# GpSimd's two waits for VectorE, before the factors and before the decay product, taken out of a 64-sequence decoder layer

## The chip, the cores and the metric

The kernel runs on one core of a Trainium2 chip. The metric is the device time of one launch in microseconds (us); lower is better. One launch computes the layer for all 64 sequences.

## The reference

Each of 64 sequences has x of 256 tokens x 256 features and a context of 120 tokens. The layer is three blocks, each with a residual and a layer norm after it:

```python
x = _layernorm(x + mamba2(x))                 # in-projection, conv, SSD scan with decay matrix, gate, out-projection
x = _layernorm(x + cross_attention(ctx, x))   # 8 heads of 64; keys and values from [context; x]
x = _layernorm(x + ffn(x))
...
# ffn
gf = _global_net(x.mean(axis=1))
out = x
for _ in range(3):
    tf = _coupling_net(out)                   # one number per token
    coupling = BASE_COUPLING + adaptive_range * (0.7 * gf + 0.3 * tf - 0.5) * 2.0
    out = out + coupling * _twist(out)        # _twist: a signed permutation of the four feature quarters
```

All data is float32. What matters here: attention ends in a division by the softmax sums (`oT * invT`), then the product with `wo`; the three cycles of the ffn are linear in x, so the kernel folds them, once the three couplings are known, into two factors per token, `out = of_x * x + of_tw * twist(x)`.

## The kernel before, in words

The four compute engines and the DMA queue each have a hand-written list of steps, and semaphores tie them together. The lists are software-pipelined over the sequences: in one turn of the main loop (61 turns, p = 2 to 62) sequence m = p is projected and scanned, a = p - 1 finishes its scan block and begins attention, f = p - 2 is in the middle of attention, f - 1 finishes attention and does its ffn, f - 2 gets its output. A turn takes some 56 us. Before and after the loop the same steps stand in lists of their own.

Names used below, by engine:

- TensorE: `turn(s, n)` (L455) transposes the probabilities of one head and token tile into a PSUM bank; `w_o(s, i)` (L482) is the output product of attention, 8 matmuls per token tile. Both take their banks from `ring_b`, which has only two, 4 and 5, in turn. In the loop the order is `turn(f, 0)`, `w_o(f - 1, 0)`, `w_o(f - 1, 1)`, `turn(f, 1)`. So `w_o(f - 1, 1)` needs the bank of `turn(f, 0)` back, and that is freed by VectorE's `turn_out(f, 0)`.
- VectorE: `divide(s, d)` (L1773) multiplies `oT` by the inverse sums, both from SBUF, in two halves; `out_x(s, i)` (L1860) and twice `out_tw(s, i, k)` (L1869) form the layer's output in `out_sb` from x2 and the factors; `turn_out` (L1764) copies a transposed tile out of PSUM. The order at the place of the change is `divide(f - 1, 0)`, `top(f, 1)` (the row maxima, L1741), `divide(f - 1, 1)`, `out_x(f - 2, 1)`, `out_tw(f - 2, 1, 0)`, `out_tw(f - 2, 1, 1)`, `turn_out(f, 0)`, `x2_raw(f - 1, 0)` (L1783).
- ScalarE: `t_col` (L1066) is the last output of the coupling net, `G` (L941) the product C B^T of the scan, and L948 and L949 make the decay matrices `Lm`, one head at a time.
- GpSimd: `masked` (L2458) masks `Lm`; `factors(s)` (L2541 to L2558) is ten tiny operations of 128x2 that make `of_x`, `of_tw`, `of_minus`; `times_g(s, q)` (L2471) multiplies two heads of `Lm` by `G`, both from SBUF, 128x384 each. The order is `masked(m, 0)` to `masked(m, 3)`, `factors(f - 1)`, `times_g(m, 0)`, `times_g(m, 1)`, and, at the head of the next turn, `times_g(a, 2)`, `times_g(a, 3)`.

One thing to watch: the turns of the engines' loops are not cut at the same moment. GpSimd's `factors(f - 1)` at the end of its turn is what VectorE's `out_x(f - 2, 1)` reads near the start of its next turn, and the second half of `divide(f)` that GpSimd's wait names is VectorE's `divide(f - 1, 1)` of its next turn. So the place of the change is one stretch of time, in which VectorE divides, waits for the factors, and forms the output.

The two waits are optional arguments: `factors(s, divided=...)` waits for `d_o`, which VectorE's two divisions raise, ahead of L2547; `times_g(s, q, summed=...)` waits for `d_out[1]`, which `out_x` and the two `out_tw` of token tile 1 raise. Neither protects data: what GpSimd touches after them is not what VectorE reads or writes before them.

Of the kernel before, what the change touches and what calls it, by code (L numbers as in the profile page):

```python
# [34 lines left out]
def decoder_layer(nc, x, xT, ctx_in, par_in, w_in, w_out, wq, wkv, wo, cw1, cw2, cw3, cw4, gw1, gw2, gw3, out):  # L35
# [25 lines left out]
    with es:  # L61
# [171 lines left out]
        def live(s):  # L233
            return 0 <= s < NSEQ
# [3 lines left out]
        def _(e):  # L238
# [220 lines left out]
            def values(s, d):  # L459
                if not live(s):  # L460
                    return
                b = bank_of["val", s, d] = take(ring_b)
                pe.wait_ge(a_v, 3 * s + 3)
                pe.wait_ge(a_tn, 8 * s + 4 * d + 4)
                pe.wait_ge(d_tn, 8 * s + 4 * d + 4)
                for c in (2 * d, 2 * d + 1):
                    at = c % 2 * L
                    for j, (_, m) in enumerate(JT):
                        for k in range(2):
                            h = 2 * c + k  # L470
                            t = mm(banks[b][k * HD:(k + 1) * HD, at:at + L], V[0:m, j, h * HD:(h + 1) * HD],  # L471
                                   probT[0:m, (8 * s + h) % HP, j, :], start=j == 0, stop=j == len(JT) - 1)
                    t.then_inc(p_val, 1)
                freed[b] = [(a_o, 2 * s + d + 1)]
# [987 lines left out]
        def _(e):  # L1462
# [3 lines left out]
            def row_stats(s, name, src, rows, done, first=0):  # L1466
                stats, _, _, _ = stat[name]
                e.bn_stats(stats[0:rows, first, :], src).then_inc(done, 1)
# [969 lines left out]
        def _(e):  # L2438
# [12 lines left out]
            def masked(s, q):  # L2451

                if not live(s):
                    return
                po.wait_ge(cum_in, 32 * s + 32)
                for c0 in (0, L):
                    pair = Lm[:, 2 * q:2 * q + 2, c0:c0 + P]
                    t = e.affine_select(out=pair, in_=pair, compare_op=ALU.is_ge, fill=MINUS, base=0, pattern=[[0, 2], [1, P]],  # L2458
                                        channel_multiplier=-1)
                t.then_inc(l_mask, 1)  # L2460

            def times_g(s, q, summed=None):

                if not live(s):
                    return
                if summed is not None:
                    po.wait_ge(d_out[1], 3 * summed + 3)
                po.wait_ge(a_G, s + 1)
                for h in (2 * q, 2 * q + 1):
                    po.wait_ge(a_dec, 8 * s + h + 1)  # L2470
                    t = tt(Lm[:, h, :], Lm[:, h, :], G[:, :], ALU.mult)  # L2471
                t.then_inc(l_Lm, 1)

            def gated(s, q):
                if not live(s):
                    return
                po.wait_ge(d_yD, 4 * s + q + 1)
                po.wait_ge(d_gate, 2 * s + 2)
                po.wait_ge(p_out, s)
                po.wait_ge(a_sq, 4 * s)  # L2480
                tt(g[:, q, :], yD[:, q, :], gate[:, q, :], ALU.mult).then_inc(l_g, 1)  # L2481

            def squares(s):
                if not live(s):
                    return
                po.wait_ge(a_sq, 4 * s + 4)
                tt(sq[:, 0:2, :], sq[:, 0:2, :], sq[:, 2:4, :], ALU.add).then_inc(l_sum, 1)
                po.wait_ge(l_sum, 2 * s + 1)
                tt(sq[:, 0, :], sq[:, 0, :], sq[:, 1, :], ALU.add).then_inc(l_sum, 1)

            def inv_rms(s):
                if not live(s):
                    return
                po.wait_ge(d_msv, s + 1)
                po.wait_ge(d_x1p, 2 * s)
                tt(rms[:, :], ms[:, :], minus_half[:, 0:TT], ALU.pow).then_inc(l_rms, 1)

            def mix(s):

                if not live(s):  # L2500
                    return
                _, mv, ve_, rs = stat["mix"]
                po.wait_ge(d_mix, 8 * s + 4)
                ts(ve_[:, 0:TT], mv[:, :, 1], EPS, None, ALU.add).then_inc(l_mix, 1)
                ts(ve_[:, TT:2 * TT], mv[:, :, 1], 1.0 + EPS, EPS * EPS, ALU.mult, ALU.add).then_inc(l_mix, 1)
                po.wait_ge(l_mix, 3 * s + 2)
                tt(rs[:, :], ve_[:, :], minus_half[:, :], ALU.pow).then_inc(l_mix, 1)

            def context(s):
                if live(s):  # L2510
                    rstd(s, "ctx", 1, J, d_ctx, l_ctx)

            def att(s, i):
                if live(s):
                    rstd(s, "att", 1, P, d_att[i], l_att[i], first=i)

            def ffn(s, i):
                if live(s):
                    rstd(s, "ffn", 1, P, d_ffn[i], l_ffn[i], first=i)

            def twist(s):

                if not live(s):
                    return
                po.wait_ge(d_f, FD * s + 3)
                tt(h_a[:, :, :], h_a[:, :, :], cpl[:, 0, :].unsqueeze(1).broadcast_to([P, KT, L]), ALU.mult).then_inc(l_tw, 1)  # L2526
                po.wait_ge(l_tw, 2 * s + 1)
                tt(h_b[:, :, :], h_b[:, :, :], h_a[:, :, :], ALU.subtract).then_inc(l_tw, 1)

            def factors(s, divided=None):  # L2530


                if not live(s):
                    return
                n = 8 * s
                po.wait_ge(d_out[0], 3 * s)
                po.wait_ge(d_out[1], 3 * s)
                for k in range(2):
                    po.wait_ge(c_in[k], 16 * (s + 1))
                c, d, e_ = (c_col[:, k, :] for k in range(3))  # L2540
                tt(cd[:, :], c, d, ALU.mult).then_inc(l_fac, 1)  # L2541
                tt(c_d[:, :], c, d, ALU.add).then_inc(l_fac, 1)
                po.wait_ge(d_base, s + 1)
                po.wait_ge(a_f, FA * s + 16)
                if divided is not None:
                    po.wait_ge(d_o, 2 * divided + 2)
                ts(e_, t_col[:, :], tf_gain[:, :], c_cyc[:, :], ALU.mult, ALU.add).then_inc(l_fac, 1)  # L2547
                po.wait_ge(l_fac, n + 3)
                ts(one_cd[:, :], cd[:, :], -1.0, 1.0, ALU.mult, ALU.add).then_inc(l_fac, 1)
                tt(e_sum[:, :], e_, c_d[:, :], ALU.mult).then_inc(l_fac, 1)  # L2550
                po.wait_ge(l_fac, n + 5)
                tt(e_one[:, :], e_, one_cd[:, :], ALU.mult).then_inc(l_fac, 1)
                po.wait_ge(l_fac, n + 6)
                tt(of_x[:, :], one_cd[:, :], e_sum[:, :], ALU.subtract)
                tt(of_tw[:, :], c_d[:, :], e_one[:, :], ALU.add).then_inc(l_fac, 1)
                po.wait_ge(l_fac, n + 7)
                ts(of_x[:, :], of_x[:, :], 1.0, None, ALU.add)
                ts(of_minus[:, :], of_tw[:, :], -1.0, None, ALU.mult).then_inc(l_fac, 1)  # L2558
# [44 lines left out]
            for p in range(2, NSEQ - 1):  # L2603
                f, a, m = p - 2, p - 1, p
                times_g(a, 2)
                times_g(a, 3)
                gated(a, 0)
                gated(a, 1)
                gated(a, 2)
                att(f - 1, 1)  # L2610
                gated(a, 3)
                att(f - 1, 0)
                squares(a)
                context(a)
                ffn(f - 2, 1)
                inv_rms(a)
                mix(a)
                twist(f - 1)
                ffn(f - 2, 0)
                masked(m, 0)  # L2620
                masked(m, 1)
                masked(m, 2)
                masked(m, 3)
                factors(f - 1, divided=f)
                times_g(m, 0, summed=f - 1)
                times_g(m, 1)
            last = NSEQ - 1
            times_g(last - 1, 2)
# [15 lines left out]
            masked(last, 1)  # L2644
            masked(last, 2)
            masked(last, 3)
            factors(last - 3, divided=last - 2)
            times_g(last, 0, summed=last - 3)
            times_g(last, 1)
            times_g(last, 2)  # L2650
            att(last - 2, 1)
# [12 lines left out]
            ffn(last - 3, 0)  # L2664
            att(last - 1, 1)
            ffn(last - 3, 1)
            factors(last - 2, divided=last - 1)
            twist(last - 1)
            ffn(last - 2, 0)
            att(last, 0)  # L2670
            att(last, 1)
            ffn(last - 2, 1)
            factors(last - 1, divided=last)
            ffn(last - 1, 1)
            twist(last)
            ffn(last - 1, 0)
# [235 lines left out]
```

## Time and profile before

| | |
|---|---|
| median of 3 runs | 3686.03 us (3682.52 to 3687.17) |
| the profiled execution | 3687.81 us, span 3685.6 us |
| TensorE clock granted, mean | 0.991 |
| TensorE matmul busy | 3613.6 us, 98% of the span |
| VectorE busy | 3246.4 us, 88% |
| ScalarE busy | 3072.9 us, 83% |
| GpSimd busy | 1788.0 us, 49% |
| chain of work that ended last | 93% TensorE, 3% VectorE, 1% each ScalarE, issue, SyncE's queue, DMA, GpSimd |

A row of a timeline tells when an instruction started, how long it took, and, in brackets, how long its engine sat idle before it and who ended that. A row of the waits tells who waited for whom, the sum over the span, how many times, and the longest.

### The profile page before, as it was taken

To read this page: it belongs to the slowest core of one execution; us is meant where nothing else is said; L and a number is where in the kernel's file an instruction comes from. 1 tells how busy PE (TensorE), PEld (TensorE's weight loads), DVE (VectorE), ACT (ScalarE), POOL (GpSimd) and SP (SyncE) were. 2 spreads that over 40 slices of the span, in tenths; PEclk is the share of its full clock that TensorE was granted. 3 is DMA by queue.
4 is the path that set the end of the run, shared out by engine and by line. 5 is a ranking of instruction groups with operands and counts; after the bars stand their busy time and mean duration, and the time that the engine had idled before them with its cause. 6 is when DMAs were issued, how large, how long until landed. Compare 5 with 4: busy or idle time off the path is not lost.

```text
span 3685.6 us, 79670 instructions
## 1 busy us (share of the span) xinstructions
PE 3613.6 (98%) x26752; PEld 3085.0 (84%) x26752; DVE 3246.4 (88%) x7970; ACT 3072.9 (83%) x7559; POOL 1788.0 (49%) x3084
## 2 busy tenths in 40 slices
PE   5999999999999999999999999999999999999997
PEld 4888888888888888888888888888888888888885
DVE  7888988988988989889889889889898898898884
ACT  5788888888888888888888888888888888888884
POOL 4355454454554554554544545545545545445442
PEclk8999999999999999999999999999999999999998
DMA  3212212112122122122121121221221221211210
GB/s 100 59 37 67 59 42 67 52 49 67 39 63 64 37 67 64 37 67 58 43 67 53 48 67 39 63 65 37 67 64 37 67 60 42 67 55 46 67 34 21
DMA packets 312358, 203.28 MB, mean 55 GB/s; under 512 B 55056, under 2 KB 310928, under 8 KB 311952
## 3 DMA queue, kind: packets, MB, share of 16 engines
q1 hardware_dynamic: 311952, 198.20, 18.7%
q8 instruction: 215, 3.52, 0.4%
q14 instruction: 191, 1.56, 0.1%
HBM read 180.17 MB, written 17.96 MB: 54 GB/s over the span
## 4 chain that ended last, share of the span: by engine, by line
PE 93%; DVE 3%; ACT 1%; issue 1%; SPq 1%; DMA 1%; POOL 1%; POOLq 0%; DVEq 0%; ACTq 0%
PE psum L263 35%; PE psum L455 10%; PE psum L471 9%; PE psum L443 8%; PE psum L350 6%; PE psum L482 6%; PE psum L518 5%; PE psum L338 5%; PE psum L524 2%; PE psum L533 2%; PE psum L322 1%; PE psum L495 1%; PE psum L383 1%; PE psum L361 1%; PE psum L545 1%
## 5 line engine op out<-in xcount | busy, mean ns | idle before, releaser
L1015 ACT ACTIVATE prob<-psum,nmax 128x376 f32<-128x376 f32 x1024 | 588.7, 582 | 36.0 <-DVE nmax L1741 35.0
L2471 POOL TENSOR_TENSOR Lm<-Lm,G 128x384 f32<-128x384 f32 x512 | 497.3, 1011 | 81.8 <-DVE out_sb L1869 68.8
L1741 DVE TENSOR_REDUCE nmax<-psum 128x2 f32<-128x752 f32 x512 | 472.8, 934 | 44.2 <-PE psum L443 39.4
L455 PE MATMUL psum<-ident,prob 128*128 128x128 f32 (+1 forms) x3072 | 486.4, 278 | 3.1 <-DVE probT L1764 1.7
L455 PEld LDWEIGHTS psum<-ident,prob 128*128 128x128 f32 (+1 forms) x3072 | 354.8, 141 | 87.0 <-issue 46.5
L1493 DVE SCALAR_TENSOR_TENSOR u<-psum,par,u 128x255 f32<-128x255 f32 (+5 forms) x960 | 408.2, 467 | 12.0 <-ACT u L914 1.5
L2458 POOL TENSOR_SCALAR_AFFINE_SELECT Lm<-Lm 128x256 f32<-128x256 f32 x512 | 193.0, 416 | 375.7 <-DMA Lm<-cum_row 375.5
L2526 POOL TENSOR_TENSOR h_a<-h_a,cpl 128x512 f32<-128x512 f32 x64 | 83.0, 1297 | 594.0 <-DVE h_pre L1852 594.0
L471 PE MATMUL psum<-probT,V 128*64 128x256 f32 (+1 forms) x3072 | 360.5, 383 | 0.4 <-ACT probT L1025 0.4
L263 PE MATMUL psum<-x_hi,w_in_hi 128*128 128x256 f32 (+1 forms) x1152 | 344.8, 299 | 13.0 <-DVE w_in_lo L1897 7.6
L263 PE MATMUL psum<-x_hi,w_in_lo 128*128 128x256 f32 (+1 forms) x1152 | 325.4, 282 | 0.0
L263 PE MATMUL psum<-x_lo,w_in_hi 128*128 128x256 f32 (+1 forms) x1152 | 324.7, 282 | 0.0
L1025 ACT ACTIVATE probT<-psum 128x384 f32<-128x384 f32 x512 | 254.7, 498 | 79.6 <-PE psum L455 72.2
L1764 DVE COPY probT<-psum 128x384 f32<-128x384 f32 x512 | 281.4, 550 | 30.4 <-PE psum L455 30.2
L471 PEld LDWEIGHTS psum<-probT,V 128*64 128x64 f32 (+1 forms) x3072 | 208.6, 136 | 110.9 <-ACT probT L1025 0.4
L948 ACT ACTIVATE Lm<-Lm,ncum 128x256 f32<-128x256 f32 x512 | 264.8, 517 | 2.6 <-DVE ncum L1605 1.9
L263 PEld LDWEIGHTS psum<-x_hi,w_in_hi 128*128 128x128 f32 (+1 forms) x1152 | 214.0, 186 | 29.6 <-issue 21.2
L350 PE MATMUL psum<-w_out_sb,g 128*128 128x256 f32 x1024 | 236.8, 384 | 1.3 <-DVE dt_a L1507 1.3
L482 PE MATMUL psum<-wo_sb,oT 128*128 128x256 f32 x1024 | 235.5, 381 | 1.7 <-DVE probT L1764 1.4
L518 PE MATMUL psum<-h,cw_sb 128*128 128x256 f32 x768 | 209.3, 395 | 10.2 <-ACT h L1058 8.4
L1015 ACT ACTIVATION_READ_ACCUMULATOR prob<-psum,nmax 128x1 f32 x1024 | 218.7, 214 | 0.0
L2481 POOL TENSOR_TENSOR g<-xc,gate 128x256 f32<-128x256 f32 x256 | 206.5, 826 | 19.5 <-DVE xc L1628 19.4
(227 smaller groups left out, 11668.6 us busy)
## 6 DMA issues: line engine op xcount, KB each, us to landing
Lm<-cum_row SPq DMA_DIRECT2D x64, 1024.0 KB, 5.2
Lm<-cum_row SPq DMA_DIRECT2D x64, 512.0 KB, 6.6
invT<-inv_row SPq DMA_DIRECT2D x256, 128.0 KB, 3.0
xT_sb<-in_xT SPq DMA_DIRECT2D x64, 256.0 KB, 2.7
x_sb<-in_x SPq DMA_DIRECT2D x64, 256.0 KB, 5.8
result<-out_sb SPq DMA_DIRECT2D x64, 256.0 KB, 2.4
inv_row<-inv_t SPq DMA_DIRECT2D x512, 1.0 KB
ctx_sb<-in_ctx SPq DMA_DIRECT2D x64, 120.0 KB, 6.4
```

Source lines behind the costliest of these rows:

```text
L263: t = mm(dst, a, b, start=n == 1, stop=n == 3 * KT)
L350: t = mm(banks[b][:, i * D:(i + 1) * D], g[:, c, i * P:(i + 1) * P], w_out_sb[:, c, :], start=c == 0, stop=c == CT - 1)
L443: t = mm(banks[at[k]][:, 0:NK], q_[r, c, i * P:(i + 1) * P], k_[r, c, :], start=m == 0, stop=m == 2)
L455: t = tr(banks[b][0:m, j * P:(j + 1) * P], prob[:, r, j0:j0 + m], ident[:, :])
L471: t = mm(banks[b][k * HD:(k + 1) * HD, at:at + L], V[0:m, j, h * HD:(h + 1) * HD], probT[0:m, (8 * s + h) % HP, j, :], start=j == 0, stop= ...
L482: t = mm(banks[b][:, 0:D], oT[:, c, i * P:(i + 1) * P], wo_sb[:, c, :], start=c == 0, stop=c == CT - 1)
L518: t = mm(b[:, 0:L], cw2_sb[:, k, :], h1[:, k, :], start=k == 0, stop=k == KT - 1)
L1015: act(prob[:, r, :], b[:, 0:NK], ACT.Exp, bias=nmax[:, n:n + 1], accum_out=psum_row[:, n:n + 1]).then_inc(a_exp, 1)
L1493: stt(u[0:rows, c, d:L], src[:, 0:L - d], prm("conv_w", 4 * c + 3 - d, slice(0, rows)), u[0:rows, c, d:L], ALU.mult, ALU.add).then_inc(don ...
L1741: e.tensor_reduce(nmax[:, 2 * n:2 * n + 2], psum[:, b:b + 2, 0:NK], AX.X, ALU.max, negate=True).then_inc(d_max, 1)
L1764: cp(probT[:, (8 * s + 2 * c + k) % HP, :, i * P:(i + 1) * P], b[:, 0:len(JT) * P].rearrange("p (j t) -> p j t", j=len(JT))).then_inc(d_tn, 1)
L2471: t = tt(Lm[:, h, :], Lm[:, h, :], G[:, :], ALU.mult)
```

## The change

GpSimd no longer waits for VectorE's two divisions inside `factors`, nor for VectorE's output sum before the first `times_g`. This is done at all five calls of `factors` that had the wait (one of them in the loop) and at both calls of `times_g` (one in the loop). No instruction is added, removed or moved on any engine; the definitions keep their optional arguments, unused.

```diff
@@ gpsimd, main loop
                 masked(m, 3)
-                factors(f - 1, divided=f)
-                times_g(m, 0, summed=f - 1)
+                factors(f - 1)
+                times_g(m, 0)
                 times_g(m, 1)
@@ gpsimd, after the loop
-            factors(last - 3, divided=last - 2)
-            times_g(last, 0, summed=last - 3)
+            factors(last - 3)
+            times_g(last, 0)
             times_g(last, 1)
@@
-            factors(last - 2, divided=last - 1)
+            factors(last - 2)
             twist(last - 1)
@@
-            factors(last - 1, divided=last)
+            factors(last - 1)
             ffn(last - 1, 1)
```

## Rows read from the trace of the kernel before

**Rows 1.** Busy time by engine, from 200 to 3400 us: us, busy us (instructions) of each.

```profile
200.00:3400.00 3200.00, 3196.59 (x23846) 2735.05 (x23844) 2875.25 (x7077) 2731.86 (x6734) 1591.94 (x2740) 1.00 0.19 55
```

**Rows 2.** Waits over the span: who <- whom, us in total, times, longest us.

```profile
DVE out_sb L1860 <- POOL of_minus L2558: 139.4, 61, 6.4
PEld psum L482 <- DVE probT L1764: 8.3, 23, 1.0
```

**Rows 3.** Timeline of VectorE in an ordinary turn: start us, us.

```profile
2147.27 0.69 DVE L1773 TENSOR_TENSOR oT<-oT,invT 128x512 f32<-128x512 f32 x1
...
2150.58 0.35 DVE L1869 SCALAR_TENSOR_TENSOR out_sb<-x,of_tw,out_sb 128x128 f32<-128x128 f32 x1
2150.85 0.34 DVE L1869 SCALAR_TENSOR_TENSOR out_sb<-x,of_minus,out_sb 128x128 f32<-128x128 f32 x1
2151.11 0.55 DVE L1764 COPY probT<-psum 128x384 f32<-128x384 f32 x1
```

**Rows 4.** Timeline of GpSimd in the same turn.

```profile
2148.18 0.34 POOL L2547 TENSOR_SCALAR c_col<-t_col,tf_gain,c_cyc 128x2 f32<-128x2 f32 x1 [3.06 <-DVE oT L1773]
...
2149.93 0.23 POOL L2558 TENSOR_SCALAR of_minus<-of_tw 128x2 f32<-128x2 f32 x1
2151.28 5.83 POOL L2471 TENSOR_TENSOR Lm<-Lm,G 128x384 f32<-128x384 f32 x6 [1.12 <-DVE out_sb L1869]
```

**Rows 5.** Timeline of ScalarE in the same turn.

```profile
2147.14 0.26 ACT L1066 ACTIVATE t_col<-psum,half_b 128x2 f32<-128x2 f32 x1
...
2149.55 0.51 ACT L941 ACTIVATE G<-psum 128x384 f32<-128x384 f32 x1
```

**Rows 6.** Timeline of TensorE: the output product in this turn and the next.

```profile
2150.20 3.62 PE L482 MATMUL psum<-wo_sb,oT 128*128 128x256 f32 x16
...
2206.17 3.62 PE L482 MATMUL psum<-wo_sb,oT 128*128 128x256 f32 x16
```

**Rows 7.** Timeline of a turn in which VectorE is late, and the next output product.

```profile
2936.14 0.55 DVE L1764 COPY probT<-psum 128x384 f32<-128x384 f32 x1
...
2934.41 1.89 PE L482 MATMUL psum<-wo_sb,oT 128*128 128x256 f32 x8
2936.74 1.99 PE L482 MATMUL psum<-wo_sb,oT 128*128 128x256 f32 x8 [0.44 <-DVE probT L1764]
...
2991.12 3.62 PE L482 MATMUL psum<-wo_sb,oT 128*128 128x256 f32 x16
```

**Rows 8.** Timeline of a turn in which TensorE and ScalarE are ahead of VectorE.

```profile
1814.33 0.35 DVE L1869 SCALAR_TENSOR_TENSOR out_sb<-x,of_tw,out_sb 128x128 f32<-128x128 f32 x1
...
1814.86 0.55 DVE L1764 COPY probT<-psum 128x384 f32<-128x384 f32 x1
...
1813.08 0.51 ACT L941 ACTIVATE G<-psum 128x384 f32<-128x384 f32 x1
...
1813.72 3.73 PE L482 MATMUL psum<-wo_sb,oT 128*128 128x256 f32 x16
```

**Rows 9.** Timeline near the end: an out_tw beside GpSimd's gated products.

```profile
3564.55 2.18 POOL L2481 TENSOR_TENSOR g<-xc,gate 128x256 f32<-128x256 f32 x3
...
3565.35 0.78 DVE L1869 SCALAR_TENSOR_TENSOR out_sb<-x,of_tw,out_sb 128x128 f32<-128x128 f32 x1
```

**Rows 10.** Timeline near the end: a times_g operation beside VectorE's x_lo.

```profile
3500.86 1.50 POOL L2471 TENSOR_TENSOR Lm<-Lm,G 128x384 f32<-128x384 f32 x1
...
3500.80 0.69 DVE L1487 TENSOR_TENSOR x_lo<-xT_sb,x_hi 128x512 fp32r<-128x512 f32 x1 [0.41 <-ACT x_hi L881]
```

**Rows 11.** Timeline: a tiny operation of factors beside one of VectorE.

```profile
461.85 0.47 POOL L2542 TENSOR_TENSOR c_d<-c_col 128x2 f32<-128x2 f32 x1
...
461.85 0.41 DVE L1541 TENSOR_TENSOR C_st<-th,C_st 16x256 fp32r<-16x256 f32 x1
```

**Rows 12.** Timeline: GpSimd's sum of squares, released by ScalarE's last square.

```profile
1828.68 0.41 ACT L955 ACTIVATE gate<-g 128x256 f32<-128x256 f32 x1
...
1829.17 1.28 POOL L2487 TENSOR_TENSOR gate<-gate 128x512 f32<-128x512 f32 x1 [0.74 <-ACT gate L955]
```

## The prediction

> **What bounds the kernel now.** First the busy times of the long middle of the run: TensorE is busy for 3196.59 of 3200 us [rows 1]. It is the bound, and only what makes it wait costs or gains anything. Then the waits over the span [rows 2]: VectorE waits 139.4 us for the factors, in 61 places, and that looks like much. Little of it reaches TensorE: its weight loads wait 8.3 us in all for VectorE's `turn_out`, in 23 places. These 8.3 us are nearly all that a faster VectorE could give back here.
>
> Last the timelines of this one place. In an ordinary turn the output product starts at 2150.20 and takes 3.62 us for its 16 matmuls [rows 6]; `turn_out` ends at 2151.11 + 0.55 = 2151.66 [rows 3], 1.46 us after that start. The next output product starts at 2206.17 [rows 6], so this turn takes 55.97 us. In a late turn `turn_out` ends at 2936.69, 2.28 us after the product's start; the second eight matmuls wait for it and start 0.05 us later; the next product starts at 2991.12, a turn of 56.71 us [rows 7]: 0.74 us more. In a third turn `turn_out` ends 1814.86 + 0.55 - 1813.72 = 1.69 us after the start and the product takes 3.73 us, 0.11 more [rows 8]. So I read a **price list**: `turn_out` done 1.5 us after the product's start costs nothing, at 1.7 us it costs 0.11, and from there each us costs a us (2.28 gives about 0.7, and the turn shows 0.74). There is 0.2 us of slack at this spot, and the bound engine stands right behind it.
>
> **What the change does, step by step.** No instruction is added or moved, so there are only times of start to work out, on the ordinary turn.
>
> 1. *The factors start earlier.* Before, L2547 starts at 2148.18, after the division's end at 2147.27 + 0.69 = 2147.96 [rows 3, 4]. Its other inputs are ready with `t_col`, at 2147.14 + 0.26 = 2147.40 [rows 5]. It then starts soon after 2147.40, in the middle of the division, which began at 2147.27. A tiny operation of GpSimd that starts together with a VectorE operation on two SBUF inputs doesn't end until 0.06 us after it (0.47 against 0.41 us) [rows 11]. So L2547 ends at 2148.02 instead of 2148.52, 0.50 us earlier. Bounds: not held at all, it ends at 2147.40 + 0.34 = 2147.74 (0.78 earlier); held for its whole length of 0.34 after the division, it ends at 2148.30 (0.22 earlier). I take 0.50, the value of the nearest row. The division itself was started first, and I charge it nothing: no division beside it is seen, and its delay would be at most a tiny operation, 0.2 us, hidden in the factors' chain of 1.64 us that follows (2148.52 to 2150.16) [rows 4].
> 2. *VectorE's output sum follows.* The first `out_tw` starts 0.42 us after the factors' end (2150.58 against 2150.16) [rows 3, 4]. It would start at 2150.08, and with nothing in its way all behind it would be 0.50 us earlier.
> 3. *But `times_g` starts earlier too.* It needs `G`, ready at 2149.55 + 0.51 = 2150.06 [rows 5], and the end of the factors, now 2149.66. GpSimd's sum of squares starts 0.08 us after the ScalarE operation that releases it (1829.17 against 1829.09) [rows 12]; with that, `times_g` starts at 2150.14 instead of 2151.28 [rows 4]. Now it stands beside the two `out_tw`, which also read two SBUF inputs, and the trace shows what that does. An `out_tw` that started 0.11 us into a product of GpSimd, the second of three, which alone stands from 3565.24 to 3565.98, took 0.78 us instead of 0.35 and ended 0.15 us after that product [rows 9]. A `times_g` operation that started 0.06 us after VectorE's `x_lo` took 1.50 us instead of 5.83 / 6 = 0.97 [rows 4] and ended 0.87 us after it [rows 10]. So one holds the other, in both directions, and who starts first goes first.
> 4. *The ordinary turn.* The first `out_tw` (2150.08) is 0.06 us ahead of `times_g` (2150.14). It ends at 2150.43, `times_g` at +0.87 = 2151.30, the second `out_tw`, held meanwhile, at +0.15 = 2151.45. `turn_out` ends 0.47 us after that (2151.66 against 2151.19 before) [rows 3]: 2151.92, or 1.72 us after the product's start. By the price list, 0.11 us. The gain of 0.50 is used up by the hold.
> 5. *The turns where VectorE is behind.* In the third turn `G` is ready at 1813.59, so `times_g` could start at 1813.67, and the first `out_tw` only at 1814.33 - 0.50 = 1813.83 [rows 8]. GpSimd is first now, and both `out_tw` are held, each behind one operation: `times_g` ends at 1814.67, `out_tw` at 1814.82, the second `times_g` at 1815.69, the second `out_tw` at 1815.84, `turn_out` at 1816.31, which is 2.59 us after the product's start. That costs 0.11 + (2.59 - 1.72) = 1.0 us. With the times of each turn put in, 17 of the 61 are of this kind; one stands in the rows.
> 6. *The sum.* 44 x 0.11 + 17 x 1.0 = 21.8 us, in place of the 8.3 us that TensorE waits now: **+13.5 us**. Turns whose division is late today (rows 7) gain, and are in this difference. Against the profiled execution, 3687.8 + 13.5 = 3701.3; the median of the runs is 1.8 us below it, so **3699 us**.
>
> What else starts earlier: all eight `times_g` end about 1 us sooner. That is worth nothing, since the products that read them stand at fixed places in TensorE's order and it was never late for want of them (3.4 us idle in 3200 [rows 1]). The cover of the one thing I cost at nothing, the tiny operations beside the division, is the chain in step 1.
>
> **A rule weighed.** Step 3 reads from [rows 9] that the hold ends before the record of GpSimd's operation does: VectorE ends 0.15 us after it, though it needs 0.35 us itself. The Trainium skill, "SBUF — State Buffer", section "Who interferes with whom" (and the section on the two separate sides), says that VectorE and GpSimd contend for one shared port pair, that it is an exclusive lock, and that whichever starts first has it for the whole instruction while the other fully blocks. It speaks against this change as the rows do, and dearer: its version is the rival "whole operations" below.
>
> **The rivals.** The measurement of this kernel tells a change of about 0.2%, 7.4 us, from none.
>
> - *GpSimd first everywhere* (slower, more). The margin of step 4 is 0.06 us. If L2547 comes only 0.22 to 0.4 us earlier, the first `out_tw` starts at 2150.18 or later, behind `times_g`, and the ordinary turn costs 1.0 us like those of step 5. Only the 11 or so turns whose division is late by a DMA keep 0.11: 50 x 1.0 + 11 x 0.11 - 8.3 = +43 us, 3729 us. For it: a thin margin. Against it: [rows 11]. Chance 0.20.
> - *Whole operations* (slower, more). Each operation holds the other until its recorded end, and the held one then needs its full length. Ordinary turn: `out_tw` to 2150.43, `times_g` to 2151.43, `out_tw` to 2151.78, `turn_out` 2152.25, 2.05 after the start, 0.44 us; early turns 0.6 us dearer, 1.55. 44 x 0.44 + 17 x 1.55 - 8.3 = +37 us, 3723 us. For it: the skill's rule named above. Against it: the 0.78 us of [rows 9]. Chance 0.10.
> - *VectorE is simply earlier* (the other side). The mechanism is step 1 without the hold of steps 3 to 5: the factors are 0.5 to 0.8 us earlier, both `out_tw` go ahead of `times_g`, or GpSimd's first operation gets in so late that `turn_out` still ends within 1.5 us of the product's start. It decides if the first `out_tw` starts before about 2150.0 and the second isn't held for more than 0.3 us. Then the 8.3 us of waits [rows 2] go and nothing comes: 3678 us; with a few of the early turns still held, 3680 to 3687. For it: 139.4 us of VectorE's waiting [rows 2] does shrink. Against it: only 8.3 us can be had. Chance 0.30, of which 0.12 by more than 0.2%.
> - My forecast, within 3690 to 3710: chance 0.40, of which some 0.07 lies within 0.2%.
>
> **The numbers.** Faster by over 0.2%: 0.12. Within 0.2%: 0.18 + 0.07 = 0.25, and slower 0.63. The likeliest case is 3699 us. The range goes from the case of all waits gone, 3678, to a little beyond the case of GpSimd first everywhere, 3735; what it leaves out is that case with the late turns too, and a gain that the 8.3 us don't explain.
>
> **What would show it.** In the profile after: L2547 released by `t_col`, about 0.5 us ahead of where it was against the output product, and ending just after the division; the first `times_g` released by `G`; one of the two `out_tw` stretched to 0.6 to 0.9 us in every turn and both in some; VectorE's wait for `of_minus` down from 2.2 to some 1.7 us a turn; TensorE's wait for `turn_out` up from 8.3 to over 15 us. I am wrong in size if both `out_tw` are long in most turns, wrong in sign if neither is.

## The result: slower by 1.75%, and the profile after

The changed kernel takes 3752.07 us (median of 4 runs, 3747.14 to 3754.92) against 3686.60 us before (4 runs): a ratio of 1.0175, with a 95% interval of 1.0163 to 1.0187. Forecast were 3699 us and a range from 3678 to 3735. The direction held; the change costs 65 us where 13.5 were forecast. The profiled executions are 3747.14 us after and 3687.81 us before, with spans of 3745.3 and 3685.6 us: 59.7 us to be explained in the traces. Where the change is described, five calls of `factors` are said to lose their wait; they are four, as its diff shows, one of them in the loop.

Busy times after, from 200 to 3400 us, in the columns of [rows 1]:

```profile
200.00:3400.00 3200.00, 3151.01 (x23429) 2685.55 (x23428) 2902.71 (x6951) 2683.96 (x6616) 1593.79 (x2693) 1.00 0.19 54
```

TensorE was idle for 3.4 us of this stretch before and for 49.0 us now. Fewer of VectorE's instructions fall into the stretch (6951 against 7077), since each turn now takes longer, and yet VectorE is busier: some of them got longer. The clock is granted in full in both.

Waits after, who <- whom, us in total, times, longest us:

```profile
DVE out_sb L1860 <- POOL of_minus L2558: 117.3, 61, 6.4
PEld psum L482 <- DVE probT L1764: 73.0, 59, 2.1
```

VectorE does wait less for the factors, 117.3 us against 139.4 [rows 2]. TensorE's weight loads wait 73.0 us for `turn_out` where it was 8.3, and in 59 places instead of 23. That is 64.7 us more, in the size of the whole loss: it comes in by the one bank.

One ordinary turn shows how. VectorE, start us, us:

```profile
1897.60 0.69 DVE L1773 TENSOR_TENSOR oT<-oT,invT 128x512 f32<-128x512 f32 x1
1900.19 0.35 DVE L1860 TENSOR_SCALAR out_sb<-x,of_x 128x256 f32<-128x256 f32 x1 [1.90 <-POOL of_minus L2558]
1900.58 1.04 DVE L1869 SCALAR_TENSOR_TENSOR out_sb<-x,of_tw,out_sb 128x128 f32<-128x128 f32 x1
1901.55 1.08 DVE L1869 SCALAR_TENSOR_TENSOR out_sb<-x,of_minus,out_sb 128x128 f32<-128x128 f32 x1
1902.55 0.54 DVE L1764 COPY probT<-psum 128x384 f32<-128x384 f32 x1
```

GpSimd in the same turn:

```profile
1897.90 0.60 POOL L2547 TENSOR_SCALAR c_col<-t_col,tf_gain,c_cyc 128x2 f32<-128x2 f32 x1 [2.90 <-ACT t_col L1066]
...
1899.93 0.23 POOL L2558 TENSOR_SCALAR of_minus<-of_tw 128x2 f32<-128x2 f32 x1
1900.47 3.98 POOL L2471 TENSOR_TENSOR Lm<-Lm,G 128x384 f32<-128x384 f32 x4 [0.31 <-ACT G L941]
```

TensorE in the same turn, and the next output product:

```profile
1900.53 1.89 PE L482 MATMUL psum<-wo_sb,oT 128*128 128x256 f32 x8
1903.15 1.99 PE L482 MATMUL psum<-wo_sb,oT 128*128 128x256 f32 x8 [0.73 <-DVE probT L1764]
...
1957.51 1.89 PE L482 MATMUL psum<-wo_sb,oT 128*128 128x256 f32 x8
```

`times_g` starts at 1900.47, 0.11 us ahead of the first `out_tw`. Both `out_tw` take 1.04 and 1.08 us instead of 0.35 and 0.34 [rows 3], each held behind one product of GpSimd. `turn_out` ends at 1903.09, 2.56 us after the output product's start; it was 1.46. The turn takes 1957.51 - 1900.53 = 56.98 us instead of 55.97 [rows 6]. Over 58 turns the output products start 57.09 us apart on the mean, before the change 56.09: a whole us a turn. The run has 59 such turns, and 59 x 1.0 us is nearly all of the 59.7 us of the spans. Of the 61 places in which the factors are waited for, 60 have both `out_tw` held, and in 5 of these `out_x` before them is held as well; a sixth `out_x` is held near the end of the run.

### The profile page after: what moved, and what is told of

The parts are those of the page before. It is cut to its first block, busy times and chain, and to the rows that moved or that the text cites. A ratio compares the mean times of both kernels' runs of the same rounds, so it can differ in the third digit from the quotient of the medians.

```text
span 3745.3 us, 79731 instructions
## 1 busy us (share of the span) xinstructions
PE 3624.1 (97%) x26752; PEld 3082.5 (82%) x26752; DVE 3330.9 (89%) x7970; ACT 3073.1 (82%) x7559; POOL 1819.1 (49%) x3084
## 4 chain that ended last, share of the span: by engine, by line
PE 85%; DVE 6%; POOL 4%; issue 4%; ACT 2%; SPq 0%; DMA 0%; POOLq 0%; ACTq 0%; DVEq 0%
PE psum L263 30%; PE psum L455 9%; PE psum L471 9%; PE psum L443 8%; PE psum L350 6%; PE psum L518 5%; PE psum L338 4%; PE psum L482 3%; PE psum L524 2%; DVE out_sb L1869 2%; PE psum L533 2%; PE psum L322 1%; POOL c_col L2547 1%; PE psum L495 1%; DVE probT L1764 1%
## 5 line engine op out<-in xcount | busy, mean ns | idle before, releaser
L2471 POOL TENSOR_TENSOR Lm<-Lm,G 128x384 f32<-128x384 f32 x512 | 509.1, 1020 | 65.6 <-ACT Lm L949 37.6
L455 PE MATMUL psum<-ident,prob 128*128 128x128 f32 (+1 forms) x3072 | 486.5, 278 | 3.2 <-DVE probT L1764 1.7
L455 PEld LDWEIGHTS psum<-ident,prob 128*128 128x128 f32 (+1 forms) x3072 | 354.8, 141 | 87.2 <-issue 46.5
L482 PE MATMUL psum<-wo_sb,oT 128*128 128x256 f32 x1024 | 247.8, 385 | 49.4 <-DVE probT L1764 49.3
L482 PEld LDWEIGHTS psum<-wo_sb,oT 128*128 128x128 f32 x1024 | 184.6, 190 | 93.8 <-DVE probT L1764 73.0
```

The costliest lines, as they stand in the source:

```text
L455: t = tr(banks[b][0:m, j * P:(j + 1) * P], prob[:, r, j0:j0 + m], ident[:, :])
L482: t = mm(banks[b][:, 0:D], oT[:, c, i * P:(i + 1) * P], wo_sb[:, c, :], start=c == 0, stop=c == CT - 1)
```

## The experiments

Ten more kernels were run, on three chips, each beside the kernel before on its own chip. The medians of before lie between 3686.9 and 3690.0 us there, so kernels of different chips are best compared by their ratios. "Held" counts the operations among `out_x` and the two `out_tw` whose record is over 0.5 us, "turn" is the mean distance of the output products over 58 turns of the profile. The one that is held in the kernel before is the `out_tw` of [rows 9], near the end of the run.

| kernel | median us | ratio to before, interval | held | turn us |
|---|---|---|---|---|
| before | 3686.6 | | 1 | 56.09 |
| the change | 3752.1 | 1.0175 (1.0163 to 1.0187) | 126 | 57.09 |
| factors free only | 3681.0 | 0.9983 (0.9974 to 0.9992) | 1 | 55.98 |
| times_g free only | 3816.2 | 1.0350 (1.0336 to 1.0364) | 181 | 58.28 |
| both, times_g behind out_x | 3704.5 | 1.0049 (1.0036 to 1.0062) | 62 | 56.39 |
| both, times_g behind first out_tw | 3680.6 | 0.9976 (0.9968 to 0.9985) | 1 | 55.98 |
| the change, shorter factors | 3707.4 | 1.0047 (1.0033 to 1.0061) | 91 | 56.48 |
| shorter factors, sum waited for | 3680.8 | 0.9976 (0.9967 to 0.9986) | 1 | 55.97 |
| the change, halves | 3698.6 | 1.0033 (1.0020 to 1.0046) | 130, shorter | 56.27 |
| the change, turn_out first | 3687.4 | 1.0002 (0.9993 to 1.0011) | 121 | 56.08 |
| before, turn_out first | 3716.2 | 1.0073 (1.0061 to 1.0086) | 1 | 56.63 |
| factors free only, turn_out first | 3715.5 | 1.0075 (1.0061 to 1.0089) | 1 | 56.58 |

### Each half of the change alone

```diff
-                factors(f - 1, divided=f)
+                factors(f - 1)
                 times_g(m, 0, summed=f - 1)
```

(and likewise at the calls after the loop, here and in the kernels below)

> Half of the change alone: factors no longer waits for the divisions, times_g still waits for the output sum. Theory (the cost is times_g holding both out_tw, and turn_out and TensorE's bank behind them): no out_tw is held, the factors still end some 0.3 us earlier, so turn_out comes 0.3 us earlier than before and most of TensorE's 8.3 us of waits go: 3679 to 3684 us. Rival (the factors beside the second division are the cost): the loss of the full change stays for the most part, 3720 to 3750 us.

Measured: 3680.97 us, 0.17% faster. The factors' half is a small gain: TensorE's wait for `turn_out` is gone from the list of waits, and a turn takes 55.98 us, the floor that the undisturbed turns of the kernel before showed.

```diff
                 factors(f - 1, divided=f)
-                times_g(m, 0, summed=f - 1)
+                times_g(m, 0)
```

> The other half alone: times_g no longer waits for the output sum, factors still waits for both divisions. Theory: times_g follows the factors at once, some 0.3 us ahead of the first out_tw, so both are held in every turn, and all of it stands 0.3 us later than in the full change because the factors do: 1.3 us a turn, 3755 to 3775 us. Where times_g catches out_x as well, another 1 us in that turn. Rival (factors beside the division): back near 3687 us.

Measured: 3816.22 us, 3.5% slower, twice the loss of the full change and 41 us over the expected range. (With the 1 us that the expectation puts on a turn in which `out_x` is caught, in 60 turns, it would have been 3815 to 3835 us.) GpSimd comes out of the factors straight into `times_g`, and catches `out_x` in every turn, not now and then. VectorE, then GpSimd, in one turn of this kernel:

```profile
1936.70 1.07 DVE L1860 TENSOR_SCALAR out_sb<-x,of_x 128x256 f32<-128x256 f32 x1 [2.25 <-POOL of_minus L2558]
1937.81 0.97 DVE L1869 SCALAR_TENSOR_TENSOR out_sb<-x,of_tw,out_sb 128x128 f32<-128x128 f32 x1
1938.70 1.08 DVE L1869 SCALAR_TENSOR_TENSOR out_sb<-x,of_minus,out_sb 128x128 f32<-128x128 f32 x1
```

```profile
1936.43 0.23 POOL L2558 TENSOR_SCALAR of_minus<-of_tw 128x2 f32<-128x2 f32 x1
1936.62 4.98 POOL L2471 TENSOR_TENSOR Lm<-Lm,G 128x384 f32<-128x384 f32 x5
```

Three operations are held in each of 60 places, and TensorE's weight loads wait 136.8 us for `turn_out`. The expectation had `times_g` 0.3 us ahead of the first `out_tw`, and so behind the start of `out_x`, which stands 0.38 us before that `out_tw`; in fact `out_x` starts 0.08 us behind `times_g`. So the two halves have opposite signs, and the wait for the output sum is what keeps the kernel fast. Without it, the free factors even help, since they give `times_g` something later to wait for (`G`): 3752 with them, 3816 without.

### The order of two starts

```diff
                 if summed is not None:
-                    po.wait_ge(d_out[1], 3 * summed + 3)
+                    po.wait_ge(d_out[1], 3 * summed + 1)
```

(with `factors` free and `summed` kept)

> The full change, but times_g waits for out_x of the same token tile (the first of the three raises of that semaphore), so it starts just behind the first out_tw. Theory (who starts first goes first): one out_tw is held instead of two, turn_out ends about 2.0 us after the output product's start instead of 2.57, 0.3 to 0.5 us a turn over the floor, 3700 to 3712 us. If out_tw is held twice all the same, 3740 us or more; if the tie is won and the second isn't held, 3682 us.

Measured: 3704.47 us. VectorE, GpSimd and TensorE in one turn of this kernel:

```profile
1880.31 0.35 DVE L1869 SCALAR_TENSOR_TENSOR out_sb<-x,of_tw,out_sb 128x128 f32<-128x128 f32 x1
1880.57 1.09 DVE L1869 SCALAR_TENSOR_TENSOR out_sb<-x,of_minus,out_sb 128x128 f32<-128x128 f32 x1
1881.58 0.54 DVE L1764 COPY probT<-psum 128x384 f32<-128x384 f32 x1
...
1880.35 2.16 POOL L2471 TENSOR_TENSOR Lm<-Lm,G 128x384 f32<-128x384 f32 x2 [0.47 <-DVE out_sb L1860]
```

`times_g` starts 0.05 us behind the first `out_tw` (0.049 before rounding) and loses; that one takes its 0.35 us. GpSimd then has its turn before the second, which ends at 1881.66. A lead of 0.11 us for GpSimd costs VectorE two holds, a lead of 0.05 us for VectorE leaves one. That is a near thing: of the 60 places with this lead, 59 go so, and in one the first `out_tw` is held all the same (1.20 us).

```diff
-                    po.wait_ge(d_out[1], 3 * summed + 3)
+                    po.wait_ge(d_out[1], 3 * summed + 2)
```

(again with `factors` free)

> The full change, but times_g waits for the first out_tw of the token tile (the second of three raises). Theory (who starts first goes first): the second out_tw has started before GpSimd learns of it, so nothing of VectorE is held; the first times_g is held 0.2 to 0.3 us instead; 3679 to 3684 us, as with the full wait. If GpSimd gets in between the two: 3695 to 3705 us.

Measured: 3680.64 us; no `out_tw` is held. The second one starts 0.16 us ahead of `times_g`. The wait need not be for the end of VectorE's last operation, only for its predecessor's.

```diff
                 tt(c_d[:, :], c, d, ALU.add).then_inc(l_fac, 1)
+                po.wait_ge(l_fac, n + 2)
+                ts(one_cd[:, :], cd[:, :], -1.0, 1.0, ALU.mult, ALU.add).then_inc(l_fac, 1)
                 po.wait_ge(d_base, s + 1)
...
-                po.wait_ge(l_fac, n + 3)
-                ts(one_cd[:, :], cd[:, :], -1.0, 1.0, ALU.mult, ALU.add).then_inc(l_fac, 1)
+                po.wait_ge(l_fac, n + 4)
                 tt(e_sum[:, :], e_, c_d[:, :], ALU.mult).then_inc(l_fac, 1)
-                po.wait_ge(l_fac, n + 5)
                 tt(e_one[:, :], e_, one_cd[:, :], ALU.mult).then_inc(l_fac, 1)
```

(on the changed kernel, both waits gone)

> The full change, with one_cd computed ahead of the wait for t_col, so that the chain from L2547 to of_minus is some 0.28 us shorter. This puts the first out_tw (4.27 us after the first division's start) ahead of times_g (4.44), as the prediction had it. Theory (the margin decides): one out_tw is held instead of two, turn_out ends 1.6 to 1.9 us after the output product's start: 3682 to 3702 us. If GpSimd goes first whatever the times, both are held: 3745 us or more.

Measured: 3707.39 us, 5 us over the expected range, but 45 us under the change. VectorE was given no further wait; it was only made earlier. The first `out_tw` is now held in 29 places instead of 60, the second still in 60. The 31 turns in which the first goes ahead are what the prediction had called ordinary; the other 29 are more than the 17 that it had counted. VectorE in one of the 31:

```profile
1884.71 0.35 DVE L1869 SCALAR_TENSOR_TENSOR out_sb<-x,of_tw,out_sb 128x128 f32<-128x128 f32 x1
1884.98 1.08 DVE L1869 SCALAR_TENSOR_TENSOR out_sb<-x,of_minus,out_sb 128x128 f32<-128x128 f32 x1
```

These turns take 56.0 to 56.1 us (all but one, the last of the loop). In 6 of the 29 others the first `out_tw` starts ahead of `times_g` as well, by 0.01 to 0.04 us, and is held all the same. VectorE and GpSimd in one of the 6:

```profile
923.87 1.20 DVE L1869 SCALAR_TENSOR_TENSOR out_sb<-x,of_tw,out_sb 128x128 f32<-128x128 f32 x1
...
923.91 1.01 POOL L2471 TENSOR_TENSOR Lm<-Lm,G 128x384 f32<-128x384 f32 x1 [0.47 <-ACT G L941]
```

So the earlier start in the profile doesn't decide the tie. In all profiles together, the 19 operations of `out_x` and `out_tw` that start 0.006 to 0.041 us ahead of the first `times_g` are held; of the 60 that start 0.048 or 0.049 us ahead, 59 are not; with a larger lead none is. VectorE has to be ahead by some 0.05 us in these records.

The same shorter factors with the sum waited for:

> The same short factors with the wait for the output sum kept (the wait for the divisions stays away). Theory: TensorE already runs at its floor of 55.97 us a turn without the shortening, so VectorE's further 0.28 us are worth nothing: 3679 to 3683 us. If VectorE's time had a value of its own here, below 3676 us.

Measured: 3680.81 us, as with the longer factors. The kernel behind the first `out_tw`, timed beside it, takes 3680.64. Once nothing is held, making VectorE earlier still is worth nothing here.

### How long a hold is

```diff
                     po.wait_ge(a_dec, 8 * s + h + 1)
-                    t = tt(Lm[:, h, :], Lm[:, h, :], G[:, :], ALU.mult)
+                    for c0 in range(0, TRI, TRI // 2 if q == 0 else TRI):
+                        cs = slice(c0, c0 + (TRI // 2 if q == 0 else TRI))
+                        t = tt(Lm[:, h, cs], Lm[:, h, cs], G[:, cs], ALU.mult)
```

(on the changed kernel)

> The full change, with each of the first two products of times_g (128x384) issued as two of 128x192. Theory (the one that is first holds the other for one whole operation and no longer): each held out_tw is then held behind half a product, some 0.45 us less each; turn_out ends about 1.7 us after the output product's start instead of 2.57, near 0.15 us a turn over the floor: 3688 to 3702 us. Rival (VectorE is kept off as long as GpSimd has products left, or the cost isn't in the length of the held operation): 3740 us or more.

Measured: 3698.61 us. All `out_tw` of this kernel, min/median/max ns:

```profile
L1869 DVE SCALAR_TENSOR_TENSOR out_sb<-x,of_tw,out_sb x128: 299/344/634, 187.1 to 3690.7; 128x128 f32<-128x128 f32 x128
L1869 DVE SCALAR_TENSOR_TENSOR out_sb<-x,of_minus,out_sb x128: 335/348/683, 187.6 to 3691.3; 128x128 f32<-128x128 f32 x128
```

60 of each are held as before, but the longest takes 0.683 us, where it was 1.087. GpSimd does the same arithmetic at the same moment, in pieces; VectorE waits for one piece at a time. That removes 53 of the 65 us (a ratio of 1.0033 instead of 1.0175) with no change of order or of any wait.

### By which way the hold reaches TensorE

```diff
                 divide(f - 1, 1)
+                turn_out(f, 0)
                 out_x(f - 2, 1)
                 out_tw(f - 2, 1, 0)
                 out_tw(f - 2, 1, 1)
-                turn_out(f, 0)
```

(on the changed kernel)

> The full change, with VectorE's turn_out(f, 0) moved ahead of out_x and both out_tw in the main loop. Theory: the holds stay (out_tw rows near 1.05 us, two in most turns), but TensorE's bank is free long before the second half of the output product; nothing but x2_raw waits behind them, with about 0.3 us to spare: 3678 to 3690 us. Rival (the collision costs in another way than by that bank, for instance by making VectorE the bound): 3730 us or more.

Measured: 3687.44 us. VectorE, then TensorE, in one turn of this kernel:

```profile
1870.47 0.97 DVE L1869 SCALAR_TENSOR_TENSOR out_sb<-x,of_tw,out_sb 128x128 f32<-128x128 f32 x1
1871.36 1.08 DVE L1869 SCALAR_TENSOR_TENSOR out_sb<-x,of_minus,out_sb 128x128 f32<-128x128 f32 x1
```

```profile
1869.34 3.62 PE L482 MATMUL psum<-wo_sb,oT 128*128 128x256 f32 x16
```

The holds are all there, and the output product runs through in 3.62 us. The 65 us of loss against the kernel before are gone. So the holds cost by what stands behind them. Against the kernel with free factors alone, timed beside it and without holds, 6.5 us are left, 0.1 us a turn (56.08 against 55.98). The waits of TensorE show where:

```profile
PEld psum L455 <- DVE x L1783: 16.6, 59, 0.3
```

`turn(f, 1)` (L455) needs the other bank of the ring, which `x2_raw` (L1783) frees, and `x2_raw` now stands right behind the two holds. The kernel with free factors alone has no such wait. That these waits are the 6.5 us was not tested.

The same move on the kernel before, with both its waits:

> The kernel before, both waits kept, with turn_out(f, 0) moved ahead of out_x and both out_tw in the main loop. Theory (the way to TensorE is the bank that turn_out frees): turn_out ends 0.76 us after the output product's start in every turn, the 8.3 us of waits go and nothing is held: 3678 to 3683 us, against 3687.4 us with the waits removed. Rival (the spot that delays TensorE in the kernel before is another): no change, 3687 us.

Measured: 3716.22 us, 0.73% slower; expected were 3678 to 3683. A miss, with a cause that shows in the waits of this kernel:

```profile
POOL Lm L2471 <- DVE out_sb L1869: 97.9, 61, 1.8
...
PEld psum L338 <- POOL Lm L2471: 39.6, 60, 1.1
```

TensorE no longer waits for `turn_out` but, in 60 turns, for `times_g`, at `y_pair` (L338). The output sum ends later behind `turn_out`, and GpSimd waits for it. GpSimd and TensorE in one turn:

```profile
1886.91 7.76 POOL L2471 TENSOR_TENSOR Lm<-Lm,G 128x384 f32<-128x384 f32 x8 [1.79 <-DVE out_sb L1869]
...
1892.17 2.17 PE L338 MATMUL psum<-Lm,xdt 128*64 128x256 f32 x24
1894.73 0.87 PE L338 MATMUL psum<-Lm,xdt 128*64 128x256 f32 x8 [0.39 <-POOL Lm L2471]
```

The eight products end at 1894.67 and the last quarter of `y_pair` starts at 1894.73. That it is the wait for the sum, and not the one for the division, was tested by the same move with `factors` free:

> factors free of the division, times_g still waiting for the output sum, turn_out(f, 0) moved ahead of out_x. Theory of the 3716 us that the same move gave with both waits: out_x comes after turn_out, so the output sum ends near 6.1 us, times_g starts at 6.2 instead of 5.6, and its last products reach TensorE's y_pair late. Out_x is bound by turn_out and not by the factors there, so freeing the factors changes nothing: 3708 to 3718 us. Rival (it was the wait for the division that cost): 3679 to 3684 us.

Measured: 3715.53 us, as expected of the former; TensorE's weight loads wait 37.8 us for `times_g` at `y_pair`, in 60 places.

## Why the prediction was wrong, point by point

- *The bound and the price list* held. In the turn shown, `turn_out` ends 2.56 us after the product's start and the turn takes 56.98 us; the list gives 55.97 + 0.11 + (2.56 - 1.72) = 56.92.
- *Step 1 failed in the size of its gain, and with it the order.* "So L2547 ends at 2148.02 instead of 2148.52, 0.50 us earlier." It does start inside the division (1897.90, with the division from 1897.60 to 1898.29), but ends at 1898.50, 0.21 us behind it and not 0.06: 0.60 us long instead of 0.34. Counted from the division's start, the end came at 0.90 us instead of 2148.52 - 2147.27 = 1.25, and since the division itself starts at the same place in the turn, the gain at this point was 0.35 us, and 0.33 at the end of `of_minus` (2.56 us behind the division's start instead of 2.89). I took the length of the hold from a tiny two-tensor operation [rows 11] and used it for one that takes 0.34 us by itself; the bound that I gave for a hold of the whole operation, 0.22 us, was as near as my value. A gain of 0.33 to 0.35 us is inside the condition of the rival "GpSimd first everywhere" (0.22 to 0.4).
- *Step 2* held: out_tw starts 0.42 us behind `of_minus` (1900.58 against 1900.16). *Step 3* held in part: `times_g` starts 0.08 us after `G`, and one operation holds the other. But "who starts first goes first" is not true to the hundredth: by the starts in the profile VectorE needs a lead of some 0.05 us.
- *Step 4 fell by step 1.* It had the first `out_tw` 0.06 us ahead; it is 0.11 us behind. A margin of 0.06 us stood on a term that I could only bound to 0.22 to 0.78, and only some 0.01 us of it lay above the lead that VectorE needs: had step 1 been right, its outcome would still have been luck. The ordinary turn costs 1.0 us instead of 0.11. Shortening the factors by hand gave the turn of step 4 back in 31 places, at 56.0 us, with VectorE 0.10 us or more ahead.
- *Step 5* held in its price (2.59 us forecast for `turn_out`, 2.56 to 2.57 found in most turns, 3.57 in the 5 with `out_x` held), but its kind is not 17 turns: it is all 59, the turns with a late division too, which step 6 let gain.
- *The sum:* 60 turns at 1.0 us, less the 8.3 us, plus the five holds of `out_x` at 1 us gives 60 x 1.0 - 8.3 + 5 = +57 us, against 59.3 between the profiled executions. The medians differ by 65.5; how many `out_x` were held in the executions without a profile isn't known.
- *The rivals.* "GpSimd first everywhere" is what happened, and had a chance of 0.20 and a time of 3729 us. Its own sum was short as well: it spared 11 turns with a late division, which are held like the others, and did not count `out_x`. "Whole operations" fell: the held `out_tw` end 0.14 and 0.15 us after GpSimd's product (1901.62 against 1901.48, 1902.63 against 1902.48), as in [rows 9], not 0.35 us after. "VectorE is simply earlier" is true of the factors' half alone: 3681 us, within the 8.3 us that it could have.
- *The range* ended at 3735 us. With a tie decided by 0.06 us, the case behind it had to be inside, together with its own next step, a hold of `out_x`.

The rule that the prediction weighed, from the Trainium skill, "SBUF — State Buffer", section "Who interferes with whom", names a mechanism: an exclusive lock on a shared port pair, for two-input operations and some one-input ones. The runs agree on the exclusion and that it lasts for one instruction; the halves show it best. They differ from it in two sizes. The held operation ends 0.14 to 0.15 us after the other's record although it needs 0.35 us itself, so the hold ends before that record does. And the earlier start decides only when VectorE's lead is at least some 0.05 us. That the two engines share a port, and not something else, is the page's account; the runs show only that they exclude each other.

## What to carry to other kernels

Before a wait between VectorE and GpSimd is taken out because no data needs it, look at what the two engines do in the next us: if both work on SBUF tensors there, the wait may be a schedule: here it was one for operations that read two such tensors, and for one that reads one. Its place can be checked by moving it one operation at a time: here a wait for the last but one operation did as well as one for the last, and a step further cost 0.5%. Where two starts lie within 0.1 us, forecast both orders and let the range hold both; and ask what stands behind the held operation, since the same holds cost 71 us against a kernel without them (3752.1 against 3681.0) with the release of a PSUM bank behind them, and 6.5 us (3687.4 against 3681.0) with it in front.

## What the runs showed of the hardware that I had not expected

- `out_x` reads only one SBUF tensor and one factor per partition, and is held all the same: 1.07 us instead of 0.35, in 60 turns of the kernel with `times_g` free only. The copy out of PSUM, `turn_out`, stands beside `times_g` in every turn and no `turn_out` of the kernel after is longer than 0.56 us; the row statistics (L1468), one SBUF input too, stay between 0.37 and 0.43 us in the kernel after.
- Between back-to-back operations of one engine the other gets its turn: the two held `out_tw` of a turn stood behind one product each, and none of the kernel after took more than 1.09 us, where a product takes about 1.
- A start in the profile that is 0.01 to 0.04 us earlier did not give VectorE its turn: all 19 such operations were held, 6 of them in the kernel with shorter factors, 9 with the halves and 4 in the kernel after.
- A tiny operation isn't held for a tiny time: L2547, 128x2, went from 0.34 to 0.60 us beside a division, and its median over all 64 is 0.606 us, where it was 0.341 before.
